# Attention with 16 heads and relative keys: near products on the two halves of TensorE's rows

## What is computed

```python
q = split_heads(x @ Wq + bq)
k = split_heads(x @ Wk + bk)
scores = jnp.einsum('bhid,bhjd->bhij', q, k)
rel = jnp.einsum('bhid,pd->bhip', q, rel_key)          # rel_key: [512, 16]
rel_idx = jnp.clip(j - i + p - 1, 0, p - 1)
bias = jnp.take_along_axis(rel, rel_idx, axis=3)
logits = jnp.where(j <= i, (scores + bias) * scale, -jnp.inf)
attn = jax.nn.softmax(logits, axis=-1)
```

## Time and profile before

| | us |
|---|---|
| median of 3 runs (lowest, highest) | 3771.6 (3763.04, 3772.19) |
| the profiled execution | 3769.35 |
| its span, first to last instruction | 3767.3 |
| PE, PEld, DVE, ACT, POOL busy, % of the span | 86, 74, 63, 39, 37 |
| attention, about | 253 to 3200 |

### The profile page before, as it was taken

One profiled execution on the slowest core, in us unless ns is written; L12 is line 12 of the kernel. 1 busy time (PEld: TensorE's weight loads), 2 busy tenths in 40 slices (PEclk: granted clock), 3 DMA queues, 4 the chain that ended last, 5 costly groups with the idle time before them and its releaser, 6 DMA issues. The chain is left out here.

```text
span 3767.3 us, 173211 instructions
## 1 busy us (share of the span) xinstructions
PE 3241.8 (86%) x76960; PEld 2785.4 (74%) x76960; DVE 2369.6 (63%) x4756; ACT 1456.2 (39%) x1765; POOL 1391.9 (37%) x1575
## 2 busy tenths in 40 slices
PE   6777999899989999998999999989999999379980
PEld 4456888787888877787888777878878777368770
DVE  8855667676366666744667677356676771465774
ACT  3631333335422333453233344622333446245551
POOL 5764323223354332225533222254332211212656
PEclk8988999999999998999999899999999999699995
DMA  4863001000311100104111000231010000544654
GB/s 128 245 173 87 29 25 39 30 17 30 108 46 41 39 30 16 30 18 121 43 30 39 30 23 24 57 95 43 30 30 16 26 13 12 166 133 144 197 171 133
DMA packets 243388, 255.20 MB, mean 68 GB/s; under 512 B 99496, under 2 KB 186380, under 8 KB 242524
## 3 DMA queue, kind: packets, MB, share of 16 engines
q1 hardware_dynamic: 222204, 202.68, 18.0%
q0 software_dynamic: 20448, 41.45, 3.6%
HBM read 151.36 MB, written 92.59 MB: 65 GB/s over the span
## 5 line engine op out<-in xcount | busy, mean ns | idle before, releaser
L959 DVE TENSOR_TENSOR att_acc<-att_pm,att_acc 128x512 f16<-128x512 f32 x1920 | 1246.3, 686 | 559.3 <-PE att_pm L1066 288.8
L1039 ACT ACTIVATE att_pt<-att_ps 128x1024 f32<-128x1024 f32 x560 | 573.2, 1024 | 1435.9 <-PE att_ps L1069 1435.9
L1066 PE MATMUL att_ps<-att_qx,table_x 68*128 68x64 f16 x8960 | 727.7, 194 | 6.2 <-issue 6.0
L1069 PE MATMUL att_ps<-att_qz,table_z 128*128 128x64 f16 x8960 | 725.0, 194 | 4.8 <-issue 4.8
L1042 ACT ACTIVATE att_pt<-att_ps 128x1024 f32<-128x1024 f32 x528 | 509.3, 1024 | 422.9 <-PE att_ps L1079 413.2
L1069 PEld LDWEIGHTS att_ps<-att_qz,table_z 128*128 128x128 f16 x8960 | 617.6, 99 | 9.3 <-issue 9.0
L1166 PE MATMUL att_po<-att_pt,att_vn 128*32 128x128 f32 x17408 | 619.2, 284 | 3.2 <-issue 2.9
L1066 PEld LDWEIGHTS att_ps<-att_qx,table_x 68*128 68x128 f16 x8960 | 614.9, 99 | 5.6 <-issue 5.0
L149 POOL TENSOR_TENSOR att_qx<-att_qe,mask_i 64x1024 f16<-64x1024 f16 x128 | 239.5, 1888 | 1026.4 <-PE att_po L1166 984.3
L1166 PEld LDWEIGHTS att_po<-att_pt,att_vn 128*32 128x32 f32 x17408 | 461.6, 113 | 59.6 <-issue 13.5
L1062 PE MATMUL att_ps<-att_qs,att_kn 113*128 113x64 f16 x8960 | 452.9, 194 | 36.9 <-DMA att_qs<-s_m 34.4
(11 more groups left out here) (211 smaller groups left out, 4081.8 us busy)
## 6 DMA issues: line engine op xcount, KB each, us to landing
att_qe<-s_q SPq DMA_DIRECT2D x256, 128.0 KB
moe_xs<-s_h SPq DMA_DIRECT2D x78, 256.0 KB
s_y<-moe_y SPq DMA_DIRECT2D x78, 256.0 KB
s_v<-att_vn SPq DMA_DIRECT2D x32, 512.0 KB, 5.3
att_vn<-s_v SPq DMA_DIRECT2D x64, 256.0 KB, 3.3
att_qs<-s_q SPq DMA_DIRECT2D x128, 66.0 KB
att_kn<-s_k SPq DMA_DIRECT2D x128, 64.0 KB, 2.5
att_x<-in_x SPq DMA_DIRECT2D x64, 128.0 KB
```

The costliest lines, as they stand in the source:

```text
L959: dve.tensor_tensor(held, got, held, ALU.max).then_inc(bank_done, 1)
L1039: act.activation(pt[:, k % 2, :, t * 64:t * 64 + 64].rearrange("p h (x c) -> p x h c", x=2), ps[t][:, :, :].rearrange("p x (h c) -> p x h ...
L1066: last = pe.matmul(groups[:, :, g], keep["table_x"][:, y:y + P], qx[0:G * D + G, s, x * (XQ // G) + g], start=False, stop=(g == XQ // G - ...
L1069: last = pe.matmul(groups[:, :, g], keep["table_z"][:, y:y + P], qz[:, s, x * (XQ // G) + g], start=False, stop=(g == XQ // G - 1), skip_g ...
```

## The change

- Near products run on row halves like the far ones. Rows 0 to 63 and 64 to 127 both hold the keys of all 16 heads (`kn` is twice as large); the halves differ in their queries, 64 each (`HQ`). A call fills two banks, each with 32 queries of 16 heads: 32 key products of 32 columns, alternating between the halves, and 16 (maxima) or 48 (exact) table products of 64 columns. It needs two free banks.
- Far products take 8 heads and 64 queries a bank: 16 products of 64 columns for two banks in place of 8 of 128.
- High and low tables are separate products on 64 rows (three in an exact group). The causal mask leaves the tables: on the diagonal an exact bank gets one product of `later` and `equal`, 512 columns, and the first maximum is bounded by `bound` in DVE.
- Values and ones take 17 columns (`VN`) in place of 32; PSUM for them is cleared once by a product with zeros.
- Loads: queries come in 8 DMAs in place of 4, groups in 32 in place of 4, in pieces of 64 queries (128 bytes). POOL spreads in two products of 128x1024 in place of four. `qs` is no longer cleared; the memset of `kn` doubles.

```diff
-SLOTS, NG = 4, P // G
+SLOTS, HQ, XQ = 4, P // 2, P // 4
+NG = HQ // G
+VN = D + 1
+QS_IN, QE_IN = 8 * 16, 8 * G * 16
...
 def load_queries(sp, io, att, n):
     s = n % SLOTS
-    for u in range(2):
-        for r, rows in ((D, 2 * D + 1), (0, D)):
-            sp.dma_start(att.qs[64 * u + r:64 * u + r + rows, s, u].rearrange("r h t -> r (h t)"),
-                         io["s_q"][n, u, 0:rows].rearrange("r h t -> r (h t)")).then_inc(att.qs_in[s], 16)
+    for half in range(2):
+        for u in range(2):
+            for r, rows in ((D, 2 * D), (0, D)):
+                sp.dma_start(att.qs[64 * half + r:64 * half + r + rows, s, u * HH:(u + 1) * HH, :],
+                             io["s_q"][n, u, 0:rows, :, half * HQ:(half + 1) * HQ]).then_inc(att.qs_in[s], 16)
 def load_groups(sp, io, att, n):
-    for part in range(2):
-        for u in range(2):
-            sp.dma_start(att.qe[64 * part:64 * part + 64, n % 2, u * HH:(u + 1) * HH].rearrange("p h t -> p (h t)"),
-                         io["s_q"][n, u, part * D:(part + 1) * D].rearrange("r h t -> r (h t)")
-                         .partition_broadcast(G)).then_inc(att.qe_in[n % 2], 16)
-def expand_groups(pool, keep, att, n, quarter):
-    s, u = n % SLOTS, quarter % 2
-    rows, dst = (G * D, att.qx) if quarter < 2 else (P, att.qz)
-    heads = slice(u * HH, (u + 1) * HH)
-    return pool.tensor_tensor(dst[0:rows, s, :, heads, :],
-                              att.qe[0:rows, n % 2, heads].rearrange("p h (g i) -> p g h i", i=G),
-                              keep["mask_i"][0:rows, :].unsqueeze(1).unsqueeze(1).broadcast_to([rows, NG, HH, G]),
+    for half in range(2):
+        for part in range(2):
+            for u in range(2):
+                for i in range(G):
+                    row = 64 * half + i * D
+                    sp.dma_start(att.qe[row:row + D, n % 2, part, u * HH:(u + 1) * HH, :],
+                                 io["s_q"][n, u, part * D:(part + 1) * D, :, half * HQ:(half + 1) * HQ]).then_inc(att.qe_in[n % 2], 16)
+def expand_groups(pool, keep, att, n, part):
+    return pool.tensor_tensor(att.qx[:, n % SLOTS, part],
+                              att.qe[:, n % 2, part].rearrange("p h (g i) -> p g h i", i=G),
+                              keep["mask_i"][:, :].unsqueeze(1).unsqueeze(1).broadcast_to([P, NG, H, G]),
                               ALU.mult)
...
                 pool.memset(keep["ident_h"][:, :], 0.0)
-                pool.memset(after[:, :], -MASK)
+                pool.memset(keep["later"][:, :, :], -1.0)
+                pool.memset(keep["equal"][:, :, :], MASK)
...
                 pool.memset(att.kn[:, :, :, :], -1.0)
-                pool.wait_ge(pool_step, 8)
...
-    step_time = {"near": 0.47, "far": 0.15, "turn": 0.44, "rows": 0.12, "norm": 0.44, "back": 0.22, "out": 0.43,
+    place_time = lambda i, j, part: 1.1 if part == 2 else 1.1 if near(i, j) else 0.25
+    step_time = {"near": 0.32, "far": 0.13, "turn": 0.44, "rows": 0.12, "norm": 0.44, "back": 0.22, "out": 0.43,
                  "turn_h": 0.22, "logit": 0.9, "count": 0.3}
...
                     if kind in ("near", "far"):
                         if kind == "near":
-                            held = acc[:, n % 2, :, r * XQ:(r + 1) * XQ]
+                            first_query = r % 2 * HQ + r // 2 * XQ
+                            held = acc[:, n % 2, :, first_query:first_query + XQ]
                             got = full[:, :].rearrange("p (h c) -> p h c", c=XQ)
                         else:
-                            first_head = r % 2 * HH + r // 2 * (HH // 2)
-                            held = acc[:, n % 2, first_head:first_head + HH // 2, :]
-                            got = full[:, :].rearrange("p (h c) -> p h c", c=P)
+                            held = acc[:, n % 2, r // 2 * HH:(r // 2 + 1) * HH, r % 2 * HQ:(r % 2 + 1) * HQ]
+                            got = full[:, :].rearrange("p (h c) -> p h c", c=HQ)
                         if behind is None:
-                            dve.tensor_scalar(held, got, LOWEST, None, ALU.max).then_inc(bank_done, 1)
+                            dve.scalar_tensor_tensor(out=held, in0=got, scalar=LOWEST,
+                                                     in1=keep["bound"][:, first_query:first_query + XQ].unsqueeze(1).broadcast_to([P, H, XQ]),
+                                                     op0=ALU.max, op1=ALU.min).then_inc(bank_done, 1)
                         else:
                             dve.wait_ge(bank_done, behind + 1)
                             dve.tensor_tensor(held, got, held, ALU.max).then_inc(bank_done, 1)
...
-                def near_scores(bank, keys, n, j, x, exact):
-                    s, rows = n % SLOTS, 64 + KM + 1
-                    pairs, groups = bank.rearrange("p (e h c) -> p e h c", e=2, h=HH), bank.rearrange("p (h g i) -> p h g i", h=H, i=G)
+                pe.matmul(po[:, :, :].rearrange("p c t -> p (c t)"), nought[:, :], keep["equal"][:, :, :].rearrange("p h c -> p (h c)"),
+                          start=True, stop=True)
+                def near_scores(banks, keys, n, j, t, exact):
+                    s, last, diagonal = n % SLOTS, [None, None], exact and n % NB == j
+                    groups = [b.rearrange("p (h g i) -> p h g i", h=H, i=G) for b in banks]
+                    for h in range(H):
+                        for e in range(2):
+                            rows = slice(64 * e, 64 * e + KM + exact)
+                            pe.matmul(banks[e][:, h * XQ:(h + 1) * XQ], keys[rows, h, :], qs[rows, s, h, t * XQ:(t + 1) * XQ],
+                                      start=(h == 0), stop=False, skip_group_check=True)
+                    if diagonal:
+                        for e in range(2):
+                            rows = slice(64 * e, 64 * e + 64)
+                            pe.matmul(banks[e], keep["later"][rows, t], keep["equal"][rows].rearrange("p h c -> p (h c)"),
+                                      start=False, stop=False, skip_group_check=True)
+                    products = ((0, 0), (1, 0), (0, 1)) if exact else ((0, 0),)
+                    for g in range(XQ // G):
+                        for table, part in products:
+                            for e in range(2):
+                                rows = slice(64 * e, 64 * e + 64)
+                                y = REL0 + 1 - G - (n % NB - j) * P - (e * HQ + t * XQ + G * g)
+                                last[e] = pe.matmul(groups[e][:, :, g], keep["table"][rows, table, y:y + P],
+                                                    qx[rows, s, part, t * (XQ // G) + g], start=False,
+                                                    stop=(g == XQ // G - 1 and table == 0 and part == exact), skip_group_check=True)
+                    return last
+                def far_scores(banks, n, j, t, exact):
+                    s, last = n % SLOTS, [None, None]
                     for h in range(HH):
-                        pe.matmul(pairs[:, :, h], keys[0:rows, h, :], qs[0:rows, s, :, h, x * XQ:(x + 1) * XQ],
-                                  start=(h == 0), stop=False, skip_group_check=True)
-                    for g in range(XQ // G):
-                        y = REL0 + 1 - G - (n % NB - j) * P - (x * XQ + G * g)
-                        last = pe.matmul(groups[:, :, g], keep["table_x"][:, y:y + P], qx[0:G * D + G, s, x * (XQ // G) + g],
-                                         start=False, stop=(g == XQ // G - 1 and not exact), skip_group_check=True)
-                        if exact:
-                            last = pe.matmul(groups[:, :, g], keep["table_z"][:, y:y + P], qz[:, s, x * (XQ // G) + g],
-                                             start=False, stop=(g == XQ // G - 1), skip_group_check=True)
-                    return last
-                def far_scores(banks, n, j, t):
-                    s, last = n % SLOTS, [None, None]
-                    for h in range(HH // 2):
                         for e in range(2):
-                            rows, head = slice(64 * e, 64 * e + KM + 1), HH // 2 * t + h
-                            last[e] = pe.matmul(banks[e][:, h * P:(h + 1) * P], kn[rows, j, head, :], qs[rows, s, e, head, :],
+                            rows, head = slice(64 * e, 64 * e + KM + exact), HH * t + h
+                            last[e] = pe.matmul(banks[e][:, h * HQ:(h + 1) * HQ], kn[rows, j, head, :], qs[rows, s, head, :],
...
                     if near(i, j):
-                        for x in range(2):
-                            last = near_scores(ps[t][:, x], kn[:, j], n, j, 2 * t + x, True)
+                        _, last = near_scores(banks, kn[:, j], n, j, t, 1)
                     else:
-                        _, last = far_scores([ps[t][:, e] for e in range(2)], n, j, t)
+                        _, last = far_scores(banks, n, j, t, 1)
...
```

(1 more changed line is left out.)

125 lines of the change are left out of this document (59 added, 66 removed).

## The result

The changed kernel takes 4424.0 us (median of 4 runs, 4412.3 to 4444.5) against 3771.9 us (4 runs, 3763.0 to 3782.1): a ratio of **1.173 [1.168, 1.179]**, 652 us slower. The forecast was 3570 us, its range 3390 to 3740. The prediction is wrong in sign; what came is its rival (c), "PE cannot be fed", to which it gave 0.12.

The account below looks back on a forecast made before the run. TensorE's stream was taken to bound attention, with VectorE next. From 3769.35 us, -346 (products) +27 (masks) +80 (VectorE waits) +8 +7 +19 (opening, projection, attention start) +4 gave 3568, or 3570 us for the median; range 3390 to 3740.

Parts of the forecast that it names:

- rival (c): Attention: TensorE cannot be fed; at 26 ns a product, 88,576 products cost 2303 us, some 4550 us in all; chance 0.12.
- the first one: Attention: TensorE is busy 92% of the time, so what its stream costs is nearly what the stage costs.
- two starts within 0.23 us: Far groups: products on two row halves start together, taken as evidence against charging instruction overhead for each half.
- The array's part: Near and far products: short pairs at 25 ns, long ones at 30, 1239 us in place of 1585.
- the saved 346 us: Near and far products in attention: the stream of products gets 346 us shorter, from 1585 to 1239 us.
- rival (a): Near key products: short pairs run as fast as their weight loads, 17 ns, 143 us less, 3425 us; chance 0.13.
- the sign that the prediction gave for it: TensorE's stream: products of a pair starting 13 ns or more apart without a wait would show the forecast wrong.
- The other sign: Near products: TensorE idle above 160 us before them would show the forecast wrong.
- Waits for DVE (+80): Near groups in attention: needing two free banks at once, TensorE waits longer for VectorE, +80 us (30 to 160).
- The opening (+8): Opening: VectorE's cast, held by GpSimd's memsets, ends later as the key memset doubles, +8 us (0 if it slips in between).
- The projection (+7, 0 to 25): Projection: 64 group load issues on queue SP take 30 us in place of 5.70 and delay stores, +7 us.
- the start of attention (+19, 8 to 35): Start of attention: more load issues on queue SP delay the row maxima that TensorE waits for, +19 us.

Follow-up runs that it names:

- e7_half: Changed kernel with half the near products, each twice as wide, so the same columns streamed: 3592.5 us, ratio 0.979 to the kernel before the change.
- e1_wide: Changed kernel with every near key and table product twice as wide, same number of instructions: 4379.2 us, ratio 1.193 to the kernel before the change.
- e2_nolow: Changed kernel without the two low table products of each exact near group, 35,840 instructions less: 3919.7 us, ratio 1.068 to the kernel before the change.

## Why the prediction was wrong, step by step

**The step that failed** is the first one, that PE's stream costs nearly what the stage costs, carried over to a stream of other density: "two starts within 0.23 us" were taken as a rate that lasts. In its place the runs show a supply of instructions of 3.9 us for 256, some 61 ns for a pair where the forecast had 28, and 563 us of stops at the ends of pages in attention.

**The array's part was right at full clock, and only there.** Pairs of 32 columns start 25.6 ns apart (forecast 25); 16 long products from 410.02 to 410.25 us are 29 ns a pair (forecast 30):

```profile
410.02 0.39 PE L1074 MATMUL att_pm<-att_qx,table 64*128 64x64 f16 x16
410.25 0.56 PE L1061 MATMUL att_ps<-att_qs,att_kn 49*128 49x32 f16 x32
```

So the 1239 us for 44,288 pairs stand as the array's work at full clock. But in the changed kernel's time the saved 346 us are not seen: without the 563 us of stops attention takes some 2890 us, and the forecast had 2626. A second term is missing there, the clock. In stretches at 1.2 GHz a pair of the exact tables takes 51 ns in place of 29 (medians of groups), and such stretches fill 998 us of attention after and 207 before. By the distances of starts in them, against the same products at full clock, they cost an estimated 249 and 69 us: 180 us that the forecast put at nothing. The other 80 or 90 us stay open. The 17 ns of rival (a) are in no trace: the weight loads of short pairs start 25 ns apart like their products.

**Rival (c) was right in mechanism, and in size by luck.** It priced a load with its product at 26 ns from the 32 value products and gave some 4550 us. From PE's restart at the start of attention to the last block's output on DVE went 3456 us in place of 2865, +591; put into (c)'s sum, 1585 + 591 - 27 = 2149 us for 88,576 products, 24 ns each. But its 26 ns are no price of supply: the groups of 32 value products keep 26 ns a product at full clock in before and in after (medians), whatever the gap of pages, so they are the pace of that work itself, while the supply gives a load with its product 30 ns at the median gap and 25 at the least. Its words, "a queue emptied in a burst", fit what the trace shows; the sign that the prediction gave for it, products of a pair 13 ns apart, does not: they start 4 ns apart, and the shortage comes as stops. The other sign did come, idle time above 160 us before near products (193.6 us before those of the maxima). Its chance could have been better: the profile of before has 616 packets of instructions, 76,960 products and loads account for 601 of them, and its trace has none closer than 3.27 us. The change makes 106,496 near and far instructions into 177,152: +276 pages, the number that came. In attention, 567 pages before and 276 more are 843 (839 came); at 3.27 us each they take 2757 us at least, and my sum had 2865 - 346 + 27 + 80 = 2626. That comes from the kernel before alone, if one takes its closest spacing for a floor, as the runs above bear out, and it excludes the forecast. At the 3.9 us that PE gets when it wants pages they take 3290; the rest up to 3456 us I put down to waits that keep pages from being wanted, which no run shows.

**Waits for DVE (+80).** Before near products of the maxima PE waits 73.0 + 10.8 us for DVE in place of 40.9 in all; before the far ones 90.5 in place of 118.6. In e7_half, where PE is less often late, they are 112 and 111 us, 64 more than before: the term was about right.

**The opening (+8) is nil.** The CAST slipped in ahead of the memset, 0.55 us, and a later operation was held in its place:

```profile
8.79 27.41 POOL L246 MEMSET att_kn<- 128x32768 f16 x1
...
32.07 5.21 DVE L289 TENSOR_SCALAR mod_raw<-mod_mag 128x2048 f32<-128x2048 f32 x1
```

It took 5.21 us in place of 1.23 and ended 1.1 us behind the memset's end at 36.20; the copies that close the stage start at 39.64 in place of 39.27 us. The text had allowed 0. The Trainium skill (SBUF — State Buffer, Who interferes with whom) has DVE and GpSimd share a port pair, held by one for a whole instruction; both lengths, 21.18 us and 5.21, agree with that.

**The projection (+7, 0 to 25) took 23**, and the start of attention (+19, 8 to 35) took 35:

```profile
128.01 41.09 SPq L144 DMA_DIRECT2D att_qe<-s_q  x64
...
172.30 1.01 PE L534 MATMUL prj_qp<-prj_hs,prj_ws 128*128 128x512 f16 x2 [25.07 <-ACT prj_qf L491]
...
390.77 0.40 PE L1061 MATMUL att_ps<-att_qs,att_kn 49*128 49x32 f16 x16 [38.58 <-DMA att_qs<-s_m]
...
1020.62 24.70 SPq L144 DMA_DIRECT2D att_qe<-s_q  x32
```

The mechanism held, the price of an issue did not: 0.64 us each for the groups, and 0.77 in block 13 (32 in 24.70 us), where I took the 0.47 of the keys, although has groups at 0.55 to 0.71. Sum before attention's steady run: 58 us, forecast 34. With 591 in attention it makes the 650 us of the two profiled executions.

**What stays open:** why pages are at least 3.2 us apart, and typically 3.7 to 3.9 when PE wants them, is not settled: a page's transfer takes 1.07 us at the median, and the rest is in no record. A direct test, more instructions without any cost of their own, wasn't found: increments cost 80 ns, one-column products 24. That it is the supply rests on the place of the stops at the ends of pages and the lock of restarts to landed pages, which no fixed cost of a product would bring; e1_wide, e7_half and e2_nolow exclude columns and DVE. Open too is why the clock fell, and what it would give back by itself.

## What to carry to other kernels

Before splitting products, count instructions: products x 2 / 256 pages, times the closest spacing of instruction packets in the trace (here 3.3 us, in steady need 3.9), is a bound beside the array's; a load with its product costs 25 to 30 ns of supply whatever it computes, so a product that the array does in less gains nothing. A burst in a timeline is no rate; look at a stretch longer than two pages. And give an added instruction a control where it should cost nothing: of the six kernels here that were to add instructions none measured the supply, and one hit the number that the theory had given. To see whether a stop is a wait for a page, number the engine's instructions: such stops fall at one place in 256.

## What I had not expected of the hardware

- Instruction pages: at least 3.2 us apart in every run; PE restarts 1.4 us after one lands, at the same place of the page in 298 of 417 stops; about two pages are held ahead.
- On one tile a product of one column costs 24 to 29 ns, nearly like one of 64; on two row halves two products start in 25.6 ns.
- A change between weights of 128 columns and of one takes 170 ns in and 100 out, at a granted clock of 0.56.
- A semaphore's increment on TensorE's queue costs 80 ns among products, at a granted clock of 0.73 to 0.75.
- The granted clock fell with the stops (0.96 to 0.85) and rose to 0.97 when the same number of products streamed twice the columns.
